# The down product of a fused MLP as three float32r products instead of one float32 product

## The reference, cut to what matters

```
mlp     = (silu(x @ gate_w) * (x @ up_w)) @ down_w          # 1024 hidden values
experts = sum over picked k of silu(x . down_embed[k]) * softmax_k * up_embed[k]   # 512 experts, 8 picks
x       = x + tanh(g_ffn) * (mlp + experts)
```

## Time and profile before

| | |
|---|---|
| median of three runs | 519.27 us (519.1 to 519.87) |
| span of the profiled execution (first to last instruction) | 517.5 us |
| PE busy | 449.8 us, 87% |
| DVE busy | 360.9 us, 70% |
| ACT busy | 246.7 us, 48% |
| POOL busy | 154.5 us, 30% |
| granted TensorE clock, mean | 0.967 of full speed |

### The profile page before, as it was taken

How to read it: one execution, slowest core, us unless ns; L and a number is a source line. 1 busy time by engine, 2 the same in 40 slices (tenths; PEclk the granted TensorE clock), 3 DMA queues, 4 the chain that set the end, 5 groups by cost and what they waited for, 6 DMA issues and landing times. The chain is left out here.

```text
span 517.5 us, 7233 instructions
## 1 busy us (share of the span) xinstructions
PE 449.8 (87%) x2142; PEld 355.1 (69%) x2142; DVE 360.9 (70%) x1034; ACT 246.7 (48%) x452; POOL 154.5 (30%) x156
## 2 busy tenths in 40 slices
PE   1617999599999889999999999898999799899991
PEld 1315688368578666878778886787777588788851
DVE  6896779995289986565987966978867554531173
ACT  3618574363576346346125315470453454955540
POOL 3955342330002131110000001032336014477771
PEclk9966999799999989999999999999999999999997
DMA  8500312000300000960000000123232423346394
GB/s 303 187 31 30 103 31 83 0 1 0 101 2 0 2 0 14 310 178 0 1 1 1 1 0 2 32 71 102 90 115 83 123 73 91 114 139 208 85 385 153
DMA packets 32965, 42.00 MB, mean 81 GB/s; under 512 B 3483, under 2 KB 26781, under 8 KB 32928
## 3 DMA queue, kind: packets, MB, share of 16 engines
q1 hardware_dynamic: 28224, 32.28, 20.7%
q0 software_dynamic: 3744, 8.42, 4.4%
q10 hardware_dynamic: 960, 0.86, 0.5%
HBM read 24.97 MB, written 18.39 MB: 84 GB/s over the span
## 5 line engine op out<-in xcount | busy, mean ns | idle before, releaser
L660 PE MATMUL acc<-w_down,act_s 128*128 128x256 f32 x384 | 92.2, 387 | 0.9 <-DVE act_s L1386 0.9
L660 PEld LDWEIGHTS acc<-w_down,act_s 128*128 128x128 f32 x384 | 74.6, 195 | 13.2 <-DVE act_s L1386 1.3
L636 PE MATMUL ring<-xt_h,up_l 128*128 128x512 f32 x160 | 70.5, 441 | 2.9 <-DVE xt_l L1356 1.5
L1601 POOL TENSOR_TENSOR rstd<-var_eps,minus_half 128x4 f32<-128x4 f32 x14 | 14.9, 1068 | 176.5 <-DVE var_eps L1186 176.5
L637 PE MATMUL ring<-xt_l,up_h 128*128 128x512 f32 x160 | 63.8, 399 | 0.0
L638 PE MATMUL ring<-xt_h,up_h 128*128 128x512 f32 x160 | 63.7, 398 | 0.0
L1098 ACT ACTIVATE act_s<-ring 128x512 f32<-128x512 f32 x48 | 28.6, 597 | 59.9 <-PE ring L638 59.6
L631 PE MATMUL ring<-small,xn 128*128 128x128 f32 x160 | 23.6, 297 | 26.2 <-ACT xn L998 14.1
L699 PE MATMUL ring<-up_e,act_s 128*128 x184 | 44.3, 383 | 2.3 <-issue 2.0
L1637 POOL DMA_INDIRECT x_rows<-main_a,slots x32 | 31.1, 971 | 43.7 <-ACT main_a L1119 34.8
L1390 DVE TENSOR_TENSOR act_s<-ring,act_s 128x512 f32<-128x512 f32 x32 | 22.0, 686 | 30.8 <-PE ring L638 21.0
(11 more groups left out here) (275 smaller groups left out, 987.8 us busy)
## 6 DMA issues: line engine op xcount, KB each, us to landing
main_b<-x_rows SPq DMA_DIRECT2D x22, 257.0 KB, 2.8
x_rows<-v_t SPq DMA_DIRECT2D x1, 3983.5 KB, 16.7
up_l<-y_rows SPq DMA_DIRECT2D x5, 512.0 KB, 7.0
stage<-in_w_mlp SPq DMA_DIRECT2D x8, 256.0 KB, 2.6
up_e<-in_w_moe SPq DMA_DIRECT2D x8, 256.0 KB, 2.6
x_rows<-v_t SPq DMA_DIRECT2D x1, 1927.5 KB, 22.8
x_nat<-in_x SPq DMA_DIRECT2D x7, 256.0 KB, 7.7
out_x<-x_nat SPq DMA_DIRECT2D x6, 256.0 KB, 5.2
```

The source lines that it names most:

```text
L636: pe.matmul(out, wl, xh, start=first, stop=False, skip_group_check=True)
L660: last = pe.matmul(acc[t // 2][:, t % 2, :], act_s[n % RING][:, tok], w_down[:, u, :], start=u == 0 and t % 2 == 0, stop=final, skip_group ...
```

## The change

`down` becomes a `three_pass` like the up products: hidden values and down weights are each split into a float32r high part and the rest, and each token tile gets three float32r products of 256 moving columns in place of one float32 product. The hidden values stay stationary and the weights moving.

The four parts are made by ACT (high) and POOL (low). In part u+1 ACT first splits the weights of unit u-2 (`split_down`, 256 columns), then the hidden values of unit u-1 (`split_hidden`, 512 columns), and then takes the silu of unit u; POOL subtracts in the same part. The low part of the hidden values lies in place over `act_s`. `down` waits for `hid_low` and `down_low`, which POOL raises; the wait on `down_done` in front of `split_down` and `split_hidden` guards two buffers of weights and three of high parts. To make room, `picks` and `exps` of the routing keep one buffer instead of one for each group, and a staging table moves.

```diff
@@ down (PE)
-                hidden_made(pe, n)
-                final = u == MLP_UNITS - 1
+                pe.wait_ge(hid_low, n + 1)
+                pe.wait_ge(down_low, n + 1)
+                first, final = u == 0, u == MLP_UNITS - 1
+                xh, xl, wh, wl = hid_h[n % LAG], hid_l[n % RING], down_h[n % 2], down_l[n % 2]
                 for t in range(GT):
                     tok = slice(t * P, (t + 1) * P)
-                    last = pe.matmul(acc[t // 2][:, t % 2, :], act_s[n % RING][:, tok], w_down[:, u, :],
-                                     start=u == 0 and t % 2 == 0, stop=final, skip_group_check=True)
+                    last = three_pass(acc[t // 2][:, t % 2, :], xh[:, tok], xl[:, tok], wh[:, :], wl[:, :],
+                                      first and t % 2 == 0, final)
@@ ACT
+            def split_down(n):
+                if n >= 2:
+                    act.wait_ge(down_done, n - 1)
+                act.activation(down_h[n % 2][:, :], w_down[:, n % MLP_UNITS, :], ACT.Copy).then_inc(down_high, 1)
+            def split_hidden(n):
+                hidden_made(act, n)
+                if n >= LAG:
+                    act.wait_ge(down_done, n - LAG + 1)
+                act.activation(hid_h[n % LAG][:, :], act_s[n % RING][:, :], ACT.Copy).then_inc(hid_high, 1)
...
                 elif kind == "mlp":
                     u = part - 1
+                    n = unit_of(g, u)
+                    if 0 <= u - 2 < MLP_UNITS:
+                        split_down(n - 2)
+                    if 0 <= u - 1 < MLP_UNITS:
+                        split_hidden(n - 1)
                     if u < MLP_UNITS:
@@ POOL
+                elif kind == "mlp":
+                    n = unit_of(g, part - 1)
+                    if 0 <= part - 3 < MLP_UNITS:
+                        pool.wait_ge(down_high, n - 1)
+                        k = (n - 2) % 2
+                        pool.tensor_tensor(down_l[k][:, :], w_down[:, part - 3, :], down_h[k][:, :].bitcast(F32),
+                                           ALU.subtract).then_inc(down_low, 1)
+                    if 0 <= part - 2 < MLP_UNITS:
+                        pool.wait_ge(hid_high, n)
+                        low = (n - 1) % RING
+                        pool.tensor_tensor(hid_l[low][:, :], act_s[low][:, :], hid_h[(n - 1) % LAG][:, :].bitcast(F32),
+                                           ALU.subtract).then_inc(hid_low, 1)
@@ buffers
-        picks = sb("picks", [P, NG, 4, TOPK + NK], BF16)
-        exps = sb("exps", [P, NG, 4, TOPK + NK + 1])
+        picks = sb("picks", [P, 4, TOPK + NK], BF16)
+        exps = sb("exps", [P, 4, TOPK + NK + 1])
```

More of the change, by code:

```diff
@@ L359, in build @@
         xt_f = xt_f_pad[:, 0:C * GN].rearrange("p (c n) -> p c n", c=C)
-        act_s = [sb(f"act_s{k}", [P, GN]) for k in range(RING)]
+        hid_l, act_s = [], []
+        for k in range(RING):
+            with nc.sbuf_tensor(f"hid_l{k}", [P, GN], F32R) as low:
+                hid_l.append(low)
+            act_s.append(sb(f"act_s{k}", [P, GN]))
+        hid_h = [sb(f"hid_h{k}", [P, GN], F32R) for k in range(LAG)]
+        down_h = [sb(f"down_h{k}", [P, D], F32R) for k in range(2)]
+        down_l = [sb(f"down_l{k}", [P, D], F32R) for k in range(2)]
         host_s = sb("host_s", [P, 2, GN])
@@ L465, in build @@
         hid_ready = sem("hid_ready")
+        hid_high = sem("hid_high")
+        hid_low = sem("hid_low")
+        down_high = sem("down_high")
+        down_low = sem("down_low")
         down_done = sem("down_done")
@@ L599, in xt_wait @@
                 eng.wait_ge(bank_full[k], turn)
-        key_iota_f = exps[:, 2:4, :, :].rearrange("p g r k -> p (g r k)")[:, 0:GN]
+        key_iota_f = kv_sum[:, NSEQ - 2:NSEQ, :].rearrange("p b m -> p (b m)")[:, 0:GN]
         sel_picks_f = kv_sum[:, NSEQ - 4:NSEQ - 2, :].rearrange("p b m -> p (b m)")[:, 0:EC * P]
@@ L804, in _ @@
                     for r in range(4):
-                        last = pe.transpose(half_words[:, r * P:(r + 1) * P], picks[:, rg, r, :], identb[:, :])
+                        last = pe.transpose(half_words[:, r * P:(r + 1) * P], picks[:, r, :], identb[:, :])
                     close_bank(key, last)
@@ L809, in _ @@
                     for r in range(4):
-                        last = pe.transpose(bank[0:TOPK + NK + 1, r * P:(r + 1) * P], exps[:, rg, r, :], ident)
+                        last = pe.transpose(bank[0:TOPK + NK + 1, r * P:(r + 1) * P], exps[:, r, :], ident)
                     close_bank(key, last)
@@ L1045, in _ @@
                     act.activation(pair_d[:, :, :], pair_d[:, :, :], ACT.Exp)
-                    act.activation(exps[:, g, :, 0:TOPK + NK], exps[:, g, :, 0:TOPK + NK], ACT.Exp).then_inc(exp_ready, 1)
+                    act.activation(exps[:, :, 0:TOPK + NK], exps[:, :, 0:TOPK + NK], ACT.Exp).then_inc(exp_ready, 1)
                 elif kind == "mlp_in" and part == 2:
@@ L1100, in _ @@
                         if u == IC:
-                            hidden_made(act, n - 1)
                             bank = full(act, (step, "EY"))
@@ L1295, in _ @@
                                       pair_top[:, :, 0:1].broadcast_to([P, 4, TOPK * TOPK]), ALU.subtract)
-                    dve.tensor_tensor(exps[:, g, :, 0:TOPK], logits[:, 0:4, 0:TOPK],
+                    dve.tensor_tensor(exps[:, :, 0:TOPK], logits[:, 0:4, 0:TOPK],
                                       top_v[:, 0:4, 0:1].broadcast_to([P, 4, TOPK]), ALU.subtract)
-                    dve.tensor_tensor(exps[:, g, :, TOPK:TOPK + NK], logits[:, 4:8, :],
+                    dve.tensor_tensor(exps[:, :, TOPK:TOPK + NK], logits[:, 4:8, :],
                                       top_v[:, 4:8, 0:1].broadcast_to([P, 4, NK]), ALU.subtract).then_inc(diff_ready, 1)
@@ L1314, in _ @@
                     with nc.allow_low_precision("counts up to 8 are exact in bfloat16"):
-                        link(dve.tensor_reduce(picks[:, g, :, 0:TOPK], hot, AX_X, ALU.add))
+                        link(dve.tensor_reduce(picks[:, :, 0:TOPK], hot, AX_X, ALU.add))
                 elif kind == "route" and part in (6, 7):
@@ L1337, in _ @@
                     zb = r_z[:, :].unsqueeze(2).broadcast_to([P, 4, TOPK])
-                    dve.tensor_tensor(exps[:, g, :, 0:TOPK], exps[:, g, :, 0:TOPK], zb, ALU.mult)
+                    dve.tensor_tensor(exps[:, :, 0:TOPK], exps[:, :, 0:TOPK], zb, ALU.mult)
                     link(dve.tensor_tensor(r_sum[:, :, :], r_sum[:, :, :], zb, ALU.mult))
```

5 lines of the change are left out of this document (2 added, 3 removed).

## The result

The changed kernel takes 559.31 us (median of four runs, 558.84 to 559.93), where the one before took 519.57 beside it: a ratio of 1.0744, 95% interval 1.0711 to 1.0777. The ratio is taken over the fast runs and is not the quotient of these two medians (1.0765): by it the change costs 38.7 us, by the medians 39.7. It is slower, as forecast, but by that much and not by 14.5, and the time lies above the range of 521 to 549. The profiled span is 557.4 us, the mean granted clock 0.928 (before: 517.5 and 0.967).

A forecast was written before the change was run, and what follows sets the result against it. PE (87% busy) bounds most of the MLP stretch, DVE the windows ahead of the spreads. Terms -7.8 + 4.6 + 4.1 + 4.0 + 1.4 + 3.2 + 5.0 = +14.5 took the span from 517.5 to 532.0, median 533.8 us, range 521 to 549.

The forecast's parts named there:

- POOL's place in the queue, and the clock: Late low parts: +4.6, +4.1, +4.0 in groups 2 and 3, +1.4 in groups 0 and 1; half clock +3.2.
- the clock: After PE's long waits the granted clock falls to nearly all 1.2 GHz: +3.2 us (0 to 7).
- the price of a product: Down on PE: a 256-column float32r product takes 0.12 us, twelve 1.44 against 1.72, saving 0.28 us a unit.
- the waits for POOL, by place and by size: PE waits for late low parts: +4.6 at group 2's end, +4.1 at group 3 unit 6, +4.0 at group 3's end.
- The 0.7 us at the ends of groups 0 and 1: After unit 8's down, a copy and three subtractions take 3.57 us against two downs of 1.44: late twice, +1.4.
- I cost them at nothing: ACT's two copies a unit, 49 us in all, covered by 59.9 us of ACT idling ahead of the silu: 0.
- 28 of 48 arrive: Four DVE-bound windows hold five downs each; those 20 savings are lost in waiting, the other 28 arrive: -7.8 us.
- where that cover is gone: Where ACT's idle time is missing, a silu comes up to 1.03 us later, and DVE's product behind it.
- DVE beside POOL: POOL instructions delay DVE's in the four DVE-bound windows, partly hidden by DVE's idle time: +5.0 us, ends 0 and 23.
- 0.17 us of DVE for each POOL instruction: One DVE loss of 1.0 us in the second window, with six POOL instructions; about ten added make 1.7 a window.
- The upper bound, 23 us: DVE's delay by POOL at most: 40 added instructions, each costing half its mean length of 1.15 us.
- Rival 3: DVE is held up two or three times as often: +10 to +18 more, some 544 to 552 us; chance 0.15.

The follow-up runs named there:

- copies alone: Changed kernel with the old float32 down and no POOL subtractions, ACT's 96 copies still made but not read: 526.75 us, ratio 1.0113 to the kernel before.
- high parts alone: Changed kernel without POOL's subtractions, the three products all reading high parts, ACT's copies kept: 524.04 us, ratio 1.0055 to the kernel before.
- fills: Changed kernel with POOL's subtractions replaced by fills of zeros, same queue places and waits: 541.32 us, ratio 1.0366 to the kernel before.
- The run with one step moved: Changed kernel with layer norm step moe_in 1 0 put behind the last two MLP parts of group 2: 551.85 us, ratio 1.0604 to the kernel before.
- the float32 down that doesn't wait: Changed kernel with the old float32 down not waiting for POOL, all copies and subtractions still made: 553.05 us, ratio 1.0597 to the kernel before.
- the run with the copies behind the silu: Float32 down, no POOL subtractions, ACT's unread copies moved below the silu of the part: 523.19 us, ratio 1.0051 to the kernel before.
- the pair with the copies behind the silu: ACT's copies below the silu, nothing on POOL: float32 down 523.19 us, ratio 1.0051; three products of high parts 520.21 us, ratio 0.9954.
- filling the stands: Changed kernel with products of zeros on PE ahead of three late downs and the routing waits of groups 0 and 1: 554.34 us, ratio 1.0653.
- the better order: Changed kernel with moe_in 1 0 behind the last two MLP parts of group 2: 551.85 us, ratio 1.0604 to the kernel before.
- Copies of 54.3 us on POOL: Changed kernel with POOL's subtractions replaced by plain copies of the high parts, reading one operand: 542.12 us, ratio 1.0369 to the kernel before.

## Why the prediction was right and wrong

Three terms failed: ACT's copies, put at nothing, cost 5.9 us; DVE's delay by POOL, put at 5.0, came to as much as 19.6; and of the cheaper product's gain 3.0 arrived for 7.8. The waits for POOL came as forecast. The terms, and what the ladder of runs gives for each (extra time by ratio, each step with those above it in place, so their sum is that of the change by the way they are taken):

| term | forecast | measured | by |
|---|---|---|---|
| ACT's copies | 0 | +5.9 (2.3 either way) | copies alone, 1.0113 |
| products, what arrives | -7.8 | -3.0 (2.5) | high parts alone, 1.0055 |
| POOL's place in the queue, and the clock | +17.3 | +16.1 (3.2) | fills, 1.0366 |
| POOL's reads beside DVE | +5.0 | +19.6 (3.5) | the change, 1.0744 |
| sum | +14.5 | +38.7 (1.7) | |

**Right: the price of a product.** 0.12 us was taken between bounds of 0.117 and 0.233; the trace shows 0.118. The Trainium skill ("TensorE: Matmul & The Clock Gate", section "Back-to-back issue gap") has a formula that gives 109 ns for 256 columns. The page gives it for an isolated product, not for a stream of weight loads and products, and the trace has 8% more, as it had for 512.

**Right: the waits for POOL, by place and by size.** Forecast were 4.6, 4.1 and 4.0 us (6.0 at most) in front of unit 11 of group 2 and units 6 and 10 of group 3; the trace shows 4.62, 4.58 and 6.65, put down to the subtraction of the weights, and the fills cost 16.1 us for a forecast of 17.3. The 0.7 us at the ends of groups 0 and 1 came once, as 1.49 at the end of group 1. The method was to walk down POOL's list and ask which older instruction waits for another engine. The run with one step moved shows it for one of them: 7.3 us. For the two of group 3 no run takes the wait alone away, and the float32 down that doesn't wait loses time there all the same, so there the size may be right partly by luck.

**Wrong: "I cost them at nothing."** The step took the 59.9 us for which ACT waits ahead of the silu as cover for the copies. But that wait ends when PE has the product, and the copy of the hidden values has a condition of its own, DVE's product of the unit before. In the windows of the earlier trace rows DVE is the late engine, so the copy stands in ACT's list waiting for DVE, and the silu, and DVE's next product, behind it. It cost 5.9 us; 3.2 of them are this order, as the run with the copies behind the silu shows. The prediction saw that a silu could come later "where that cover is gone", but gave it no price; that a queue stands still where its next instruction waits it asked of POOL and not of ACT. For the other 2.6 us the cause isn't shown.

**Mis-sized: "28 of 48 arrive".** The rule was right in kind: in the pair with the copies behind the silu, the four windows are 117.2 us long with the float32 down and 118.1 with the products, so nothing is gained inside them. But the count was misread. The records of the down in the windows of the earlier trace rows, in the kernel before (busy us and records of PE, then of weight loads, clock, DMA share, GB/s):

```profile
75.90:97.70 21.80, 5.79 (x25) 4.54 (x24) 0.93 0.15 49
150.20:183.00 32.80, 9.44 (x40) 7.58 (x40) 1.00 0.00 1
245.00:272.00 27.00, 6.35 (x28) 4.79 (x26) 1.00 0.00 1
321.60:357.00 35.40, 7.55 (x32) 6.07 (x32) 1.00 0.21 66
```

At eight records to a unit these 125 are less than 16 units, not 20. By its own rule some 32 units, 9 us, should have arrived; 5.0 did (3.0 with the copies ahead of the silu), and 2.9 of the difference are PE's waits for ACT's copies.

**Mis-sized: DVE beside POOL, 5.0 us for 19.6.** This is the largest error, 14.6 of the 24.2 us. What failed first is the rate: 0.17 us of DVE for each POOL instruction came from one loss in one window; in the four windows POOL has 33 more instructions (20 in the earlier trace rows, 53 after) and DVE 12.7 more busy us, 0.38 each. And the step counted these windows only, where 12.4 of the 17.9 us between the profiles of fills and change lie; 5.5 lie elsewhere. The upper bound, 23 us, did hold the value. Rival 3, at a chance of 0.15, was this mechanism with the right price: it gave +10 to +18 more, and 14.6 more came. Alone that would have ended at 548.4, inside the range; what carried the time past 549 are ACT's copies (5.9) and the gain that didn't arrive (4.8).

The Trainium skill ("SBUF — State Buffer", section "Who interferes with whom") says that a VectorE instruction with two SBUF inputs contends with a GpSimd instruction that reads SBUF and not with one that only writes. The runs agree: 896 ns in the median under subtractions, 691 under fills, and at most 692 for the product that reads PSUM. The page also names tensor_scalar as one that can take the shared ports. Line 1230 can't show that here: it reaches 1512 ns in the changed kernel and took at most 930 before, but it also reaches 1251 with ACT's copies alone, where POOL subtracts nothing. The prediction used the rule, and by it came to 5.1, with the last two windows losing about half of what the first two lose. DVE's busy time grows by 3.8, 3.0, 3.4 and 2.5 us in the four: the rule says who is held up, not how often.

**Near: the clock.** 3.2 us were forecast; filling the stands gave 4.7, give or take 2.3, with those ahead of the spreads included. After each of the three waits the granted clock is 0.50 to 0.53, as foreseen.

No version of the change that makes and reads the low parts came near the kernel before: 551.85 with the better order is the best of them. Even with the low parts left out and the copies in their better place the gain is 0.5%.

## What to carry to other kernels

When work is moved to an engine that is idle half the time, go through each engine's list and ask of every new instruction what it waits for and what stands behind it; idle time ahead of one instruction is no cover for another with a condition of its own. An engine whose instructions hold up those of the bounding engine is not free even where nothing waits for it: price it by the bounding engine's instructions that can be held up, over the whole span, and from more than one case in the trace. And a gain on the fullest engine counts only up to its next wait for the engine that is late; how many units lie ahead of such a wait is counted in the trace.

## What the runs showed of the hardware

POOL's subtraction of 128 x 512 float32 takes 1337 ns, a copy of the same size 674, and the copies, which hold DVE up much less, cost the kernel no more than fills do (1.0369 and 1.0366). Copies of 54.3 us on POOL lengthen DVE by 4.2 us over fills, subtractions of 103.0 us by 20.0. The loss falls on few instructions: 41 of 1034 are over 0.1 us longer, nearly 0.6 us each.

Missing clock was cheap in these runs: 17 us of full clock given back came with 4.7 us of time in the changed kernel.
